# Two attention layers' statistics on GpSimd, keys and values ahead of a wait, and a quarter one product later

## What is computed

```
x = x + L0(gn(x));  x = x + L1(gn(x))         # gn: group norm over 32 groups of 4 channels
L0: v = round(clip(x,-1,1)*127)/127*0.6;  f = v + 0.1*v^3
    outs[i] = conv3x3(f, g_pos[i]-g_neg[i]),  i = 0..2
    result = (adc(o0)*4 + adc(o1)*2 + adc(o2)*1 + adc(o2))*factor + bias   # adc: scale, round, clip
L1: q,k,v = Wq x, Wk x, Wv x;  ek = exp(k)
    out = Wm ( q * (exp(B) (ek*v)) / (exp(B) ek) )
```

## Time and profile before

| | |
|---|---|
| median of 3 runs | 1522.66 us (1522.54 to 1523.33) |
| the profiled execution | 1522.15 us, of which the span of the page 1520.4 us |
| busy: PE, DVE | 1430.8 us (94%), 1400.2 us (92%) |
| busy: ACT, POOL | 1193.8 us (79%), 528.1 us (35%) |
| chain that ended last | DVE 51%, PE 25%, issue 16%, ACT 5% |
| mean granted TensorE clock | 0.983 of full speed |

### The profile page before, as it was taken

The page is one execution under the profiler, slowest core; times in us unless marked ns, Lnnn a source line. Parts: engine busy times, 40 slices in busy tenths (PEclk is TensorE's granted clock), DMA queues, the critical chain, the costliest instruction groups (busy, mean ns, idle before and its releaser), DMA issues.

```text
span 1520.4 us, 24553 instructions
## 1 busy us (share of the span) xinstructions
PE 1430.8 (94%) x8560; PEld 659.2 (43%) x8560; DVE 1400.2 (92%) x2185; ACT 1193.8 (79%) x1561; POOL 528.1 (35%) x503
## 2 busy tenths in 40 slices
PE   2799999999999999999999999999999999999975
PEld 2444444444444444444444444444444444444432
DVE  6879999999999999999999999999999999999766
ACT  4547788788978878897887889788797978876563
POOL 3111334333433433343343334434333443433312
PEclk9799999999999999999999999999999999999997
DMA  5011011223123222312322231232223123212232
GB/s 209 1 56 42 15 29 46 94 56 111 35 56 105 57 84 56 111 39 56 101 56 84 56 112 37 53 108 56 84 56 112 32 56 108 57 28 57 56 84 84
DMA packets 29181, 103.92 MB, mean 68 GB/s; under 512 B 4032, under 2 KB 4224, under 8 KB 29056
## 3 DMA queue, kind: packets, MB, share of 16 engines
q1 hardware_dynamic: 20416, 70.86, 12.6%
q0 software_dynamic: 8640, 31.46, 10.9%
HBM read 37.29 MB, written 33.55 MB: 47 GB/s over the span
## 4 chain that ended last, share of the span: by engine, by line
DVE 51%; PE 25%; issue 16%; ACT 5%; DVEq 1%; POOL 1%; DMA 0%; SPq 0%; ACTq 0%; POOLq 0%
PE A L504 5%; PE A L506 4%; PE A L505 4%; DVE duo L1135 4%; DVE A L1198 3%; DVE A L1207 3%; DVE uall L1201 3%; DVE uall L1228 3%; DVE duo L1195 3%; DVE uall L1203 3%; DVE A L1199 3%; DVE duo L1196 3%; DVE f L1112 2%; PE B L504 2%; DVE t L1147 2%
## 5 line engine op out<-in xcount | busy, mean ns | idle before, releaser
L504 PE MATMUL A<-T,WH 128*128 128x504 f16 (+1 forms) x1152 | 438.5, 381 | 0.0
L505 PE MATMUL A<-T,WH 128*128 128x504 f16 (+1 forms) x1152 | 437.5, 380 | 0.0
L506 PE MATMUL A<-T,WL 128*128 128x504 f16 (+1 forms) x1152 | 437.5, 380 | 0.0
L1525 POOL TENSOR_TENSOR T<-t,T 128x512 f16<-128x512 f32 x189 | 259.5, 1399 | 421.8 <-ACT T L769 421.8
L1499 POOL TENSOR_TENSOR zl<-z,zh 128x512 f16<-128x512 f32 x120 | 160.5, 1354 | 404.9 <-ACT zh L880 404.9
L812 ACT ACTIVATE junk<-xr,shift 128x1024 f16<-128x1024 f32 x244 | 280.1, 1148 | 5.4
L504 PE MATMUL B<-T,WH 128*128 128x504 f16 (+1 forms) x576 | 222.0, 385 | 19.9 <-DVE T L1161 11.5
L505 PE MATMUL B<-T,WH 128*128 128x504 f16 (+1 forms) x576 | 221.9, 385 | 0.0
L506 PE MATMUL B<-T,WL 128*128 128x504 f16 (+1 forms) x576 | 221.8, 385 | 0.0
L504 PEld LDWEIGHTS A<-T,WH 128*128 128x128 f16 x1152 | 115.4, 100 | 165.5 <-issue 47.6
L506 PEld LDWEIGHTS A<-T,WL 128*128 128x128 f16 x1152 | 112.7, 98 | 136.2
(11 more groups left out here) (186 smaller groups left out, 2573.0 us busy)
## 6 DMA issues: line engine op xcount, KB each, us to landing
xr<-in_x_dram SPq DMA_DIRECT2D x64, 512.0 KB, 5.7
out_dram<-xr SPq DMA_DIRECT2D x64, 512.0 KB, 2.7
xr<-shared POOLq DMA_DIRECT2D x60, 512.0 KB, 4.5
xr<-in_L_conv_g_pos_dram SPq DMA_DIRECT2D x3, 576.0 KB, 9.9
xr<-in_L_conv_g_neg_dram SPq DMA_DIRECT2D x3, 576.0 KB, 10.9
xr<-in_L_conv_Wm_dram SPq DMA_DIRECT2D x2, 32.0 KB, 9.0
xr<-in_L_conv_Wq_dram SPq DMA_DIRECT2D x1, 32.0 KB, 11.7
xr<-in_L_conv_Wk_dram SPq DMA_DIRECT2D x1, 32.0 KB, 11.6
```

Source lines behind the costliest of these rows:

```text
L504: nc.tensor.matmul(to, wh, th, start=fresh and y == 1, stop=False, skip_group_check=True)
L505: nc.tensor.matmul(to, wh, tl, start=False, stop=False, skip_group_check=True)
L506: done = nc.tensor.matmul(to, wl, th, start=False, stop=y == 2, skip_group_check=True)
L1525: last = nc.gpsimd.tensor_tensor(low, t32[:, pair, :, :, :].rearrange("p t e w -> p (t e w)"), high, ALU.subtract)
```

## The change

It has three parts. First, `spread_stats` goes from VectorE's list to GpSimd's, as six instructions with a wait ahead of five (a sum over four columns becomes two additions); the second one stands in slot 11 instead of 12. At the head of the program the first four of the five stay on VectorE and the last one goes to ScalarE. Second, `keys_values` is called before the wait on `m2_copied`, in every quarter; `queries`, which writes pair B, stays behind it. Third, in the tables, quarter 1 moves: keys and values on TensorE and the exponential on ScalarE from slot 32 to 33, the sums from 33 to 34 on TensorE, from 34 to 35 on ScalarE, the ratio and the addition from 35 to 36.

```diff
@@ tables
-KV_PE = (21, 32, 39, 45)
-SUMS_PE = (22, 33, 40, 46)
-KV_ACT = (21, 32, 39, 44)
-SUMS_ACT = (23, 34, 41, 45)
+KV_PE = (21, 33, 39, 45)
+SUMS_PE = (22, 34, 40, 46)
+KV_ACT = (21, 33, 39, 44)
+SUMS_ACT = (23, 35, 41, 45)
-SUMS_DVE = (24, 35, 42, 49)
+SUMS_DVE = (24, 36, 42, 49)
-ADD_POOL = (35, 42, 49, 60)
+ADD_POOL = (36, 42, 49, 60)
-X1_SPREAD = 12
+X1_SPREAD = 11
@@ second_layer, TensorE
+                if values:
+                    keys_values(values[0], values[2], 0)
                 if values or mixed:
...
                 if values:
-                    keys_values(values[0], values[2], 0)
                     queries()
@@ head, ScalarE
+            act.wait_ge(mask_made, 1)
+            act.wait_ge(averaged[0], 2)
+            nc.scalar.activation(gin[0][:, 0:GROUP], mask[:, :], ACT.Identity, scale=chan[0][:, :]
+                                 ).then_inc(spread[0], 1)
@@ VectorE: spread_stats becomes spread_head (image 0 alone, without its last instruction)
-                nc.vector.tensor_scalar(gin[which][:, 0:GROUP], mask[:, :], chan[which][:, :], None, ALU.mult
-                                        ).then_inc(spread[which], 1)
-                    if nxt and slot == X_SPREAD:
-                        spread_stats(0, p + 1)
-                    if prev and slot == X1_SPREAD:
-                        spread_stats(1, p - 1)
@@ last_sums, VectorE
+                dve.wait_ge(spread[1], B - 1)
@@ GpSimd
+            def spread_stats(which, image):
+                N = float(H * W)
+                if isinstance(image, int) and image == B - 1 and which:
+                    pool.wait_ge(tail_moments, 2)
+                waits_apart(pool, (stats_in[which], nth(image, NG, NG - 1)), (passed[which], nth(image, NG, NG - 1)))
+                nc.gpsimd.tensor_tensor(pairs[which][:, :, :], moments[which][:, :, 0:2], moments[which][:, :, 2:4],
+                                        ALU.add).then_inc(paired[which], 1)
+                waits_apart(pool, (paired[which], nth(image, 1, which - 1)))
+                nc.gpsimd.tensor_tensor(total[which][:, :], pairs[which][:, :, 0], pairs[which][:, :, 1], ALU.add
+                                        ).then_inc(totalled[which], 1)
+                waits_apart(pool, (totalled[which], nth(image, 1, 0)))
+                nc.gpsimd.tensor_scalar(mean[which][:, :], total[which][:, 0:1], 1.0 / N, None, ALU.mult
+                                        ).then_inc(averaged[which], 1)
...
+                waits_apart(pool, (averaged[which], nth(image, 2, 1)))
+                nc.gpsimd.tensor_scalar(gin[which][:, 0:GROUP], mask[:, :], chan[which][:, :], None, ALU.mult
+                                        ).then_inc(spread[which], 1)
@@ phase, GpSimd
                     second_layer(p, m, slot, images)
+                    if nxt and slot == X_SPREAD:
+                        spread_stats(0, p + 1)
+                    if prev and slot == X1_SPREAD:
+                        spread_stats(1, p - 1)
```

More of the change, by code:

```diff
@@ L179, in conv_layers_kernel @@
         moments = [sb(f"moments{i}", [P, 2, NG]) for i in range(2)]
+        pairs = [sb(f"pairs{i}", [P, 2, NG // 2]) for i in range(2)]
         total = two("total", [P, 2])
@@ L290, in conv_layers_kernel @@
         passed = [sem("passed0"), sem("passed1")]
+        paired = [sem("paired0"), sem("paired1")]
         totalled = [sem("totalled0"), sem("totalled1")]
@@ L1071, in head_sums, with spread_head @@
                 dve.wait_ge(head_moments, 3)
-            def spread_stats(which, image):
+            def spread_head():
                 N = float(H * W)
[L1077 to L1086, removed]
-                                               op0=ALU.mult, op1=ALU.subtract)
-                nc.vector.tensor_scalar(chan[which][:, :], mean[which][:, :], shift[which][:, :], None, ALU.subtract
-                                        ).then_inc(averaged[which], 1)
-                dve.wait_ge(averaged[which], nth(image, 2, 1))
-                nc.vector.tensor_scalar(gin[which][:, 0:GROUP], mask[:, :], chan[which][:, :], None, ALU.mult
-                                        ).then_inc(spread[which], 1)
@@ new lines, in spread_head @@
+                dve.wait_ge(stats_in[0], NG)
+                dve.wait_ge(passed[0], NG)
+                nc.vector.tensor_reduce(total[0][:, :], moments[0][:, :, :], mybir.AxisListType.X, ALU.add
+                                        ).then_inc(totalled[0], 1)
+                dve.wait_ge(totalled[0], 1)
+                nc.vector.tensor_scalar(mean[0][:, :], total[0][:, 0:1], 1.0 / N, None, ALU.mult
+                                        ).then_inc(averaged[0], 1)
+                dve.wait_ge(averaged[0], 1)
@@ L1094, in group_moments @@
+                nc.vector.scalar_tensor_tensor(out=gin[0][:, GROUP:GROUP + 1], in0=total[0][:, 0:1],
+                                               scalar=mean[0][:, :], in1=total[0][:, 1:2],
+                                               op0=ALU.mult, op1=ALU.subtract)
+                nc.vector.tensor_scalar(chan[0][:, :], mean[0][:, :], shift[0][:, :], None, ALU.subtract
+                                        ).then_inc(averaged[0], 1)
             def group_moments(which, image):
@@ L1419, in _ @@
             head_sums()
-            spread_stats(0, 0)
+            spread_head()
             group_moments(0, 0)
@@ L1464, in weight_difference @@
                 nc.gpsimd.tensor_tensor(gi, gi, gn[:, i * CK:(i + 1) * CK], ALU.subtract).then_inc(w_diff, 1)
+            def spread_stats(which, image):
[11 more added lines that the diff above has]
+                                        ).then_inc(averaged[which], 1)
+                waits_apart(pool, (averaged[which], nth(image, 2, 0)))
+                nc.gpsimd.tensor_scalar(chan[which][:, :], mean[which][:, :], shift[which][:, :], None, ALU.subtract
+                                        ).then_inc(averaged[which], 1)
+                nc.gpsimd.tensor_scalar(gin[which][:, GROUP:GROUP + 1], total[which][:, 0:1], mean[which][:, :],
+                                        total[which][:, 1:2], ALU.mult, ALU.subtract)
+                waits_apart(pool, (averaged[which], nth(image, 2, 1)))
+                nc.gpsimd.tensor_scalar(gin[which][:, 0:GROUP], mask[:, :], chan[which][:, :], None, ALU.mult
+                                        ).then_inc(spread[which], 1)
             def inverse_std(which, image):
```

## The result

The changed kernel takes 1531.25 us (median of 4 runs, 1530.6 to 1534.32), the kernel before 1522.64. The ratio is 1.006, with a 95% interval of 1.0042 to 1.0077: slower, where the prediction had 1521.5 and a range up to 1527. The profiled execution took 1530.6 us, its span is 1528.8 us, 8.4 more than before.

What follows compares the result with a forecast made beforehand. TensorE was nearly full, with some 1.2 us a phase to give. Head -1.6, the 13 phases +0.3 and the last changed phase +0.1 gave -1.2 us: 1520.95 profiled, 1521.5 as median; 8-in-10 range 1514 to 1527.

Steps and rivals of the forecast that it cites:

- T to S: From the second transformed quarter being ready (T) to the start of quarter 1's sums (S): 3.15 us instead of 0.82.
- S to R: From the sums' start to the start of product 1 in the next phase's slot 2 (R): 7.39 us, before 8.82.
- R's wait: Product 1 in the next phase's slot 2 would wait half a microsecond for ScalarE's rounding, previously done 0.88 us ahead.
- G to M: From the second group matmul's start (G) to the third step's mix on VectorE (M): 0.98 us instead of 1.81.
- T to R: Second transformed quarter ready to product 1 in the next phase's slot 2: 10.54 us against 9.64 before.
- Keys and values ahead of the wait: Quarter 1 on TensorE: the 0.51 us wait for the copy to m2 goes; hardly any in other quarters.
- GpSimd at nothing: GpSimd's six small instructions per statistics set, 2.1 us a set, costed at nothing; uncovered up to 2.1 us a phase.
- The -1.6: Head: GpSimd goes on 1.6 us earlier, first turned weights near 21; 1.6 us off, bounds 0.3 and 2.4.
- The waits did not simply go: Rival: TensorE's 19.1 us of waits for m2's copy and the weighted values vanish, giving 1503 us; 4 in 100.
- ScalarE did not reach the rounding in time: Milder rival: ScalarE rounds in time, so product 1 needn't wait; phase 88.0 us, total 1515; 25 in 100.
- the port: Rival: GpSimd's small instructions block VectorE over the shared SBUF port, giving the time back; 1529 us, 17 in 100.
- The slower outcome: Whole kernel slower by more than 0.2% (3.05 us): 21 in 100, 17 from the shared port, 4 from the forecast's own mechanism.

Runs made afterwards that it cites:

- queries_ahead: The changed kernel with the copy of quarter 1's queries alone taken ahead of the casts on ScalarE: 1521.72 us, ratio 1.0009.
- statistics_alone: The kernel before with the change's first part alone (small statistics on GpSimd, the head's last one on ScalarE): 1511.2 us, ratio 0.9927.
- keys_alone: The kernel before with the second part alone, keys and values called ahead of the wait for the copy to m2: 1522.21 us, ratio 1.0004.
- second_set_alone: The kernel before with the head's change and only the second, cheap set of statistics (slot 11) on GpSimd: 1511.92 us, ratio 0.994.
- head_alone: The kernel before with the head's change alone, the last of image 0's five small instructions on ScalarE: 1520.72 us, ratio 1.0001.
- later_alone: The kernel before with the third part alone, quarter 1 a product later: 1552.51 us, ratio 1.0203.
- exp_alone_ahead: The changed kernel with quarter 1's exponential alone taken ahead of the casts on ScalarE: 1527.82 us, ratio 1.004.

## Why the prediction was wrong

**T to S, the step that failed.** "... the weighted values 0.68, and two hand-overs ... That is T to S 3.15 us instead of 0.82." The chain was followed from the exponential to the sums, but what stands in front of the sums on TensorE was not: the final product of quarter 0, which writes pair B and needs the copy of quarter 1's queries out of it. The copy moved behind the casts together with the exponential, and the prediction counted its length in ScalarE's list for R, but not who waits for it. 3.83 was measured; with the copy alone put ahead of the casts (`queries_ahead`) it is 3.13. The 0.68 us, passed on to R and 13 times, are 8.8 of the 11 us that the 13 phases were off; of the other 2.2, 1.3 are the remaining 0.1 in each clean phase, and 0.9 lie in the difference between a clean phase and the mean. The trace says where: the first five phases take 89.30 to 89.32 us, the later ones 89.48 and the ninth 90.36. Why is not shown.

**S to R, and R's wait.** Right: 7.42 for 7.39, and R waits 0.40 us for the rounding (13 times, 5.8 us). Since ScalarE is what R waits for, nothing of the 0.68 could be made good.

**G to M.** Right (0.99). By `statistics_alone` it is worth 0.80 us a phase, 11 us in all; the one cheap set gives nearly all of it. With the casts in the next slot the change could have had 1.02 (88.61 - 87.59).

**The third part's price.** The prediction had T to R 0.90 longer. By runs it is 1.65 us a phase as made (89.48 - 87.83), and 0.93 with the copy out of the way (88.76 - 87.83). The 0.90 was therefore right for all but the copy.

**Keys and values ahead of the wait.** The wait went, as said; worth nothing, shown by `keys_alone`.

**GpSimd at nothing.** Right. Six instructions take 2.05 us in the first set (601.38 to 603.43) against 2.1 estimated, and 2.67 us in the second (the first and the last of its six rows below), which ends at 610.65, 3.1 us before the group matmul at 613.78:

```profile
607.98 0.58 POOL L1474 TENSOR_TENSOR pairs<-moments 128x4 f32<-128x4 f32 x1 [4.55 <-ACT junk L815]
...
610.34 0.31 POOL L1488 TENSOR_SCALAR gin<-mask,chan 128x4 f32<-128x4 f32 x1
```

**The head.** The -1.6 did not come. The statistics were ready earlier, as said (GpSimd's step at 14.91 instead of 15.98), but the first turned weights came at 23.29, not near 21. The prediction had the reason as its lower bound, "the next subtraction falls on VectorE's sums": there L1031 took 2.93 us instead of 0.55. Without these 2.4 us they would have come at 20.9, an estimate. And even that would not have been a gain by itself, since TensorE's first product did not follow them.

That the profiled run reached 167.24 rather than 170.35 is TensorE's clock, which was less often at the lower of its two levels. Stretch 60 to 100, before and then after:

```profile
60.00:100.00 40.00, 34.58 (x150) 17.83 (x151) 28.01 (x47) 19.09 (x28) 8.88 (x10) 0.84 0.14 53
```

```profile
60.00:100.00 40.00, 33.73 (x158) 17.78 (x159) 29.37 (x45) 20.93 (x30) 10.95 (x16) 0.96 0.15 53
```

In both kernels TensorE idles 2.43 us and then 3.8 to 3.9 us, with only 12 small matmuls between, up to 63.43 (before) and 64.16 (after), and its matmuls then take 0.61 to 0.64 us instead of 0.38, at 1.2 instead of 2.4 GHz. In the changed kernel that ends at 67.1. Before, it ends at 69.0 and returns at 86.1 to 89.0, behind 1.99 us of idling, and once more at 137.5 to 140.0; the changed kernel idles 1.99 us at the same place and stays at the higher level. The edits do not decide this: `statistics_alone` and `second_set_alone` have the same head, a clock of 0.84 and 0.96 in this stretch, and reach the first pair at 170.98 and 167.34. `head_alone` has 0.96 and 167.23. So the -3.1 us of the first stretch does not belong to the change, and it hides that much of the 11.3 us that the phases lost.

**The rivals.** The waits did not simply go, ScalarE did not reach the rounding in time, and in the phases the port took nothing back. The slower outcome had 21 in 100, most of it for the port; a slip in a chain of hand-overs across engines had 4. The range up to 1527 allowed 0.1 us on each link, and not a link that was missing.

## What to carry to other kernels

When a piece moves past others in an engine's list, follow every instruction of it to its next reader, and a copy that frees a buffer to the next writer of that buffer: the one that frees it can be later than the one that computes. Put small instructions that others wait for into the gap ahead of a long one's input, not behind the long one; here one number in a table was worth 24 us. A wait in the list of waits of the engine that is bound says where time is seen, not that it can be had: look at what stands next in line.

## What the hardware showed

A short wait can cost more than itself. In `later_alone` TensorE waits 2.4 to 2.9 us ahead of the final product in each phase, and in eight of the 13 phases its clock falls to the lower of its two levels, 1.2 GHz, right behind it. TensorE in one of them:

```profile
580.47 1.09 PE L639 MATMUL B<-shared,wmf 64*64 64x256 f32 x16 [2.52 <-issue]
581.35 1.66 PE L617 MATMUL L<-shared,eb 64*64 64x256 f32 x16
582.95 0.61 PE L504 MATMUL A<-T,WH 128*128 128x512 f16 x1
...
585.30 0.38 PE L504 MATMUL A<-T,WH 128*128 128x504 f16 x1
```

Sixteen matmuls take 1.66 us instead of 1.10, and those of 512 columns 0.61 instead of 0.38. In this phase R comes at T + 12.33 (589.85) instead of 11.25, about 1.1 us on top of the wait. In the changed kernel, with waits of 1.71 to 1.81 us and 2.58 in the first phase, no matmul of the 13 phases was that slow. The length of the wait alone does not decide: 2.86 us in the tenth phase of `later_alone` had no slow matmul behind it, 2.10 in the first of `exp_alone_ahead` had (sixteen in 2.01 us).

An instruction of VectorE beside one of GpSimd can take several times its own time. At the head that held for the small one (2.54 us before, 0.23 in `keys_alone`, where GpSimd's subtraction started only at 13.31) and for the sum of 128x384 (2.92 us instead of 0.55). Taking VectorE's work away moved the meeting instead of ending it. For GpSimd's twelve small instructions in a phase no such loss is seen: `statistics_alone` has them all and 87.81 us, `second_set_alone` half of them and 87.86.
